# The first layer's weights are normalised after the values product; their reciprocals are widened, transposed and multiplied into the context

## The reference

```python
q = hidden @ Wq + bq                      # 32 heads of 16
k = enc @ Wk + bk; v = enc @ Wv + bv      # 8 key/value heads of 16
attn = softmax(q k^T / sqrt(16) + mask)
out = (attn @ v) @ Wo + bo
x = layer_norm(out + hidden) * gamma + beta
```

## Time and profile before

| what | value |
|---|---|
| median of three runs | 2440.0 us |
| the profiled execution | 2442.29 us, of which the span on the core is 2440.3 |
| busy TensorE, its weight loads | 2361.1 us (97%), 2030.8 us (83%) |
| busy VectorE, ScalarE, GpSimd | 1215.0 (50%), 868.8 (36%), 814.0 (33%) us |
| chain that ended last | TensorE 86%, GpSimd 7%, VectorE 3%, ScalarE 2% |
| granted TensorE clock | 0.992 of full speed |

### The profile page before, as it was taken

One profiled execution on the slowest core, in us unless ns is written; L12 is line 12 of the kernel. 1 busy time (PEld: TensorE's weight loads), 2 busy tenths in 40 slices (PEclk: granted clock), 3 DMA queues, 4 the chain that ended last, 5 costly groups with the idle time before them and its releaser, 6 DMA issues.

```text
span 2440.3 us, 38739 instructions
## 1 busy us (share of the span) xinstructions
PE 2361.1 (97%) x14768; PEld 2030.8 (83%) x14768; DVE 1215.0 (50%) x2041; ACT 868.8 (36%) x2501; POOL 814.0 (33%) x597
## 2 busy tenths in 40 slices
PE   7998999999999999999988899999999999999999
PEld 5777888888888888878866788888888888887887
DVE  6985333434533334465679843343354333334654
ACT  7964222222422222342379532222233222223321
POOL 6964232233322223130059442233243322322100
PEclk9999999999999999999999999999999999999999
DMA  5002111112110101211320021111111110110110
GB/s 206 10 10 83 35 43 52 37 48 67 35 35 34 43 34 43 74 44 61 115 85 6 10 83 44 48 46 52 34 57 35 36 41 34 43 52 14 61 44 35
DMA packets 37764, 120.06 MB, mean 49 GB/s; under 512 B 3616, under 2 KB 3872, under 8 KB 37664
## 3 DMA queue, kind: packets, MB, share of 16 engines
q1 hardware_dynamic: 37664, 118.69, 14.0%
HBM read 114.48 MB, written 4.19 MB: 49 GB/s over the span
## 4 chain that ended last, share of the span: by engine, by line
PE 86%; POOL 7%; DVE 3%; ACT 2%; issue 2%; DMA 0%; SPq 0%; POOLq 0%; DVEq 0%; ACTq 0%
PE PS L574 72%; PE PS L803 5%; PE PS L819 4%; PE PS L811 2%; POOL XN L429 1%; POOL W L453 1%; POOL HF L429 1%; POOL X L463 1%; POOL P0D L429 1%; POOL XN L422 1%; ACT AT L1147 1%; PE PS L794 1%; POOL W L386 1%; ACT PS L1147 1%; PE PS L839 0%
## 5 line engine op out<-in xcount | busy, mean ns | idle before, releaser
L574 PE MATMUL PS<-AT,W 128*128 128x512 f32 x2496 | 603.6, 392 | 7.1 <-DVE AT L1441 6.9
L574 PEld LDWEIGHTS PS<-AT,W 128*128 128x128 f32 x2496 | 467.8, 189 | 110.2 <-DVE AT L1441 9.8
L492 POOL TENSOR_TENSOR PR<-PR,RC 128x512 f32<-128x512 f32 x128 | 133.5, 1043 | 979.3 <-DVE RC L1528 979.3
L1320 DVE TENSOR_TENSOR X<-PS,X 128x512 f32<-128x512 f32 x416 | 286.0, 690 | 295.5 <-PE PS L574 288.4
L574 PE MATMUL PS<-CT,W 128*128 128x512 f32 x1632 | 408.9, 399 | 10.9 <-DVE CT L1315 10.5
L574 PE MATMUL PS<-W,CX 128*128 128x512 f32 x1632 | 397.2, 397 | 6.7 <-DVE Q L1345 4.0
L574 PE MATMUL PS<-W,CT 128*128 128x256 f32 x3072 | 385.9, 284 | 0.0
L574 PEld LDWEIGHTS PS<-W,CT 128*128 128x128 f32 x3072 | 372.9, 191 | 1.3 <-issue 0.8
L574 PEld LDWEIGHTS PS<-W,CX 128*128 128x128 f32 x1632 | 299.9, 188 | 74.0 <-issue 7.1
L574 PEld LDWEIGHTS PS<-CT,W 128*128 128x128 f32 x1632 | 298.8, 189 | 69.8 <-issue 11.6
L1174 ACT ACTIVATE CX<-PS,VEC 128x512 fp32r<-128x512 f32 x128 | 88.1, 689 | 660.9 <-PE PS L819 660.8
(11 more groups left out here) (110 smaller groups left out, 2462.0 us busy)
## 6 DMA issues: line engine op xcount, KB each, us to landing
RAW<-in_wq SPq DMA_DIRECT2D x44, 512.0 KB, 4.5
RAW<-in_wo SPq DMA_DIRECT2D x44, 512.0 KB, 3.2
RAW<-in_wk SPq DMA_DIRECT2D x40, 512.0 KB, 3.3
RAW<-in_wv SPq DMA_DIRECT2D x40, 512.0 KB, 3.4
raw_c<-in_cT SPq DMA_DIRECT2D x8, 512.0 KB, 6.0
raw_x<-in_xT SPq DMA_DIRECT2D x8, 512.0 KB, 5.7
BVR<-in_bv_rows SPq DMA_DIRECT2D x8, 512.0 KB, 3.6
X<-in_x SPq DMA_DIRECT2D x4, 1024.0 KB, 11.1
```

Of the source, the lines that this page charges most:

```text
L492: nc.gpsimd.tensor_tensor(PR[:, :, 0:P], PR[:, :, 0:P], RC[:, 0, 0:BT].unsqueeze(2).to_broadcast([P, BT, P]), ALU.mult).then_inc(norm_done, 1)
L574: ins = nc.tensor.matmul(out, lhs(c, a), rhs(c, b), start=(k == 0), stop=(k == total - 1))
L1320: V_.tensor_tensor(X[:, tile, :], PS[:, bank, :], X[:, tile, :], ALU.add).then_inc(done, 1)
```

## The change

In layer 0, GpSimd no longer multiplies the exponentials by the reciprocals before their transposition. The exponentials are transposed as they are. GpSimd adds the two halves of each of the last three heads (`half`), so that VectorE's sum over them reads 192 numbers a row and not 384, and it widens the eight reciprocals to 128 columns (`widen`), which TensorE transposes (`rt0`) into columns 256 to 383 of a score bank. When a unit's context has been evicted raw (`cxraw0`), VectorE multiplies it by the four transposed reciprocals (`cxnorm0`), and GpSimd makes its high and low part (`context`); for the last unit ScalarE and VectorE do (`last_cxlo0`). The value bias is added when the values are evicted. `RC` and `SUM0` have four slots, not two; the widened reciprocals and half sums lie in the upper half of the value-bias rows. The additions to X go between mask addition and maximum; `rec0` moves behind `soft0`; rows, bias tiles, quarters, the first keys and values of the next layer and the layer norm's first parts go to other steps. The diff, cut:

```diff
-    12: (2, (0,)), 13: (2, (1,)), 14: (2, (2,)), 15: (2, (3,)), 20: (1, (0, 1)), 21: (1, (2, 3)),
-    22: (3, (0,)), 23: (3, (1,)), 24: (3, (2, 3)), 25: (0, (0,)), 26: (0, (1,)), 27: (0, (2,)), 28: (0, (3,))}
+    11: (2, (0,)), 13: (2, (1,)), 15: (2, (2,)), 16: (2, (3,)), 17: (1, (0,)), 18: (1, (1,)), 20: (1, (2,)), 21: (1, (3,)),
+    23: (3, (0, 1)), 24: (3, (2, 3)), 26: (0, (0,)), 27: (0, (1,)), 28: (0, (2,)), 29: (0, (3,))}
-BO_AT = {8: 0, 9: 1, 10: 2, 11: 3, 16: 4, 17: 5, 18: 6, 19: 7}
-ROWS_AT = {9: (0, 0), 10: (0, 1), 11: (0, 2), 13: (0, 3), 17: (1, 0), 18: (1, 1), 19: (1, 2), 21: (1, 3),
-   25: (2, 0), 26: (2, 1), 27: (2, 2), 28: (2, 3)}
+BO_AT = {8: 0, 9: 1, 10: 2, 11: 3, 12: 4, 13: 5, 16: 6, 20: 7}
+ROWS_AT = {10: (0, 0), 11: (0, 1), 13: (0, 2), 14: (0, 3), 18: (1, 0), 19: (1, 1), 21: (1, 2), 22: (1, 3),
+   26: (2, 0), 27: (2, 1), 28: (2, 2), 29: (2, 3)}
...
+CXF = in_arena("CXF", [P, 3, 2, BTOK], F32, 36864)
...
+HS = BVR[:, 1024:1024 + (KV0 - OWN) * P].rearrange("p (s h t) -> p s h t", s=2, t=P // 2)
+RC0 = BVR[:, 1536:2048].rearrange("p (s n) -> p s n", n=P)
...
-        def norm(s):
+        def half(s):
+            pool.wait_ge(exp0, hf * STEPS0 + (s + 1))
+            if s >= 2:
+                pool.wait_ge(rc0, hf * STEPS0 + (s - 1))
+            z = P0[s % BUFS0].rearrange("p (h t) -> p h t", t=P)[:, OWN:KV0, :]
+            nc.gpsimd.tensor_tensor(HS[:, s % 2, :, :], z[:, :, 0:P // 2], z[:, :, P // 2:P], ALU.add).then_inc(half0, 1)
+        def widen(s):
             pool.wait_ge(rc0, hf * STEPS0 + (s + 1))
-            z = P0[s % BUFS0].rearrange("p (h t) -> p h t", t=P)
-            nc.gpsimd.tensor_tensor(z, z, RC[:, s % 2, :].unsqueeze(2).to_broadcast([P, KV0, P]),
-                                    ALU.mult).then_inc(norm0, 1)
+            if s >= 4:
+                pool.wait_ge(rt_ps, hf * STEPS0 + (s - 3))
+            copy_hi(RC0[:, s % 4, :].rearrange("p (h d) -> p h d", d=HD0),
+                    RC[:, s % 4, :].unsqueeze(2).to_broadcast([P, KV0, HD0])).then_inc(wide0, 1)
+        def context(u):
+            pool.wait_ge(cx0_n, hf * UNITS0 + (u + 1))
+            copy_hi(CX0[:, u % 3, 0, :], CXF[:, u % 3, 1, :]).then_inc(cx0_hi, 1)
+            pool.wait_ge(cx0_hi, hf * UNITS0 + (u + 1))
+            nc.gpsimd.tensor_tensor(CX0[:, u % 3, 1, :], CXF[:, u % 3, 1, :], CX0[:, u % 3, 0, :].bitcast(F32),
+                                    ALU.subtract).then_inc(cx0_lo, 1)
 
...
         sub(2)
+        half(0)
         for s in range(STEPS0):
-            if s + 1 < STEPS0:
-                norm(s + 1)
             if s == STEPS0 - 2:
                 sub_rows(0, 0)
             if s + 3 < STEPS0:
                 sub(s + 3)
+            if s + 1 < STEPS0:
+                half(s + 1)
+            widen(s)
+            if s % 4 == 1 and s > 1:
+                context(s // 4 - 1)
             if s in BO_AT:
...
         def t0(s):
-            pe.wait_ge(norm0, s0 + (s + 1))
+            pe.wait_ge(exp0, s0 + (s + 1))
...
             elif b == 0:
-                pe.wait_ge(cx0_lo, u0 + u)
+                pe.wait_ge(cx0_raw, u0 + u)
...
+        def rt0(s, bank, col):
+            pe.wait_ge(wide0, s0 + (s + 1))
+            nc.tensor.transpose(PS[:, bank, col:col + P], RC0[:, s % 4, :],
+                                IDENT[:]).then_inc(rt_ps, 1)
...
                 pv0(s - 1)
+            if s and s <= STEPS0 - 4:
+                pe.wait_ge(z0, s0 + (s + 4))
+                if s % 4 == 1 and s > 1:
+                    pe.wait_ge(cx0_n, u0 + s // 4)
+                rt0(s - 1, B0 + (s - 1) % 4, 256)
             if s + 4 < STEPS0:
                 s0_(s + 4)
...
             if s in ROWS_AT:
                 out0(s)
-            if s == STEPS0 - 4:
-                pe.wait_ge(z0, s0 + STEPS0)
+            if s == STEPS0 - 3:
+                pe.wait_ge(cx0_n, u0 + UNITS0 - 1)
                 keys(n1, 0, 0, w1, BS)
-            if s == STEPS0 - 3:
+            if s == STEPS0 - 2:
                 values(n1, 0, w1, None, (0, 1))
-            if s == STEPS0 - 2:
+            if s == STEPS0 - 1:
                 values(n1, 0, w1, None, (2, 3))
-            if s == STEPS0 - 1:
-                keys(n1, 0, 1, w1, BS + 1)
+        keys(n1, 0, 1, w1, BS + 1)
...
+        pe.wait_ge(cx0_lo, u0 + UNITS0 - 1)
         last_rows0(0, 0)
+        pe.wait_ge(xadd, x0 + 3 * BT)
         last_rows0(1, 0)
         pv0(STEPS0 - 1)
+        for t in range(BT):
+            rt0(STEPS0 - BT + t, BPV, t * P)
         pe.wait_ge(k_ev, n1 * 2 + 2)
         last_rows0(2, 0)
...
-            nc.scalar.activation(VT[:, tb, :], PS[:, BB, :], ACT.Copy).then_inc(vt_ev, 1)
+            nc.scalar.activation(VT[:, tb, :], PS[:, BB, :], ACT.Identity, bias=VEC[:, COL_BV0:COL_BV0 + 1]).then_inc(vt_ev, 1)
...
         def e0(s):
...
-            if s >= 2:
-                act.wait_ge(rc0, s0 + (s - 1))
+            if s >= 4:
+                act.wait_ge(rc0, s0 + (s - 3))
...
-                                     bias=MX[:, s % BUFS0, h:h + 1], accum_out=SUM0[:, s % 2, h:h + 1])
+                                     bias=MX[:, s % BUFS0, h:h + 1], accum_out=SUM0[:, s % 4, h:h + 1])
...
-        def cxhi0(u):
+        def cxraw0(u):
...
-            nc.scalar.activation(CX0[:, u % 3, 0, :], PS[:, BB, :], ACT.Identity,
-                                 bias=VEC[:, COL_BV0:COL_BV0 + 1]).then_inc(cx0_hi, 1)
+            nc.scalar.activation(CXF[:, u % 3, 1, :], PS[:, BB, :], ACT.Copy).then_inc(cx0_raw, 1)
...
             if s == 0:
...
             if s % 4 == 0 and s:
-                cxhi0(s // 4 - 1)
+                cxraw0(s // 4 - 1)
             if s + 3 < STEPS0:
...
-            if s == STEPS0 - 4:
+            if s == STEPS0 - 3:
                 first_keys(0, BS)
-            if s == 30:
+            if s == 31:
                 root(hf * 8)
         first_keys(1, BS + 1)
-        cxhi0(UNITS0 - 1)
+        cxraw0(UNITS0 - 1)
+        act.wait_ge(cx0_n, u0 + UNITS0)
+        nc.scalar.activation(CX0[:, (UNITS0 - 1) % 3, 0, :], CXF[:, (UNITS0 - 1) % 3, 1, :], ACT.Copy).then_inc(cx0_hi, 1)
         root(hf * 8 + 1)
...
-        def soft0(s):
+        def soft0(s, row=None):
...
+            if row is not None:
+                row0(row)
             dve.wait_ge(z0, s0 + (s + 1))
             V_.tensor_reduce(MX[:, s % BUFS0, :], P0[s % BUFS0].rearrange("p (h t) -> p h t", t=P),
                              AXX, ALU.max, negate=True).then_inc(max0, 1)
...
+        def row0(s):
+            n, t = ROWS_AT[s]
+            if n < 2:
+                dve.wait_ge(bo_tile, hf * SEQ + (n * BT + t + 1))
+            add0(n, t, BA)
...
-            V_.tensor_reduce(SUM0[:, s % 2, OWN:KV0], P0[s % BUFS0].rearrange("p (h t) -> p h t", t=P)[:, OWN:KV0, :],
-                             AXX, ALU.add).then_inc(sum0, 1)
-            if s >= 2:
-                dve.wait_ge(norm0, s0 + (s - 1))
+            dve.wait_ge(half0, s0 + (s + 1))
+            V_.tensor_reduce(SUM0[:, s % 4, OWN:KV0], HS[:, s % 2, :, :], AXX, ALU.add).then_inc(sum0, 1)
+            if s >= 4:
+                dve.wait_ge(wide0, s0 + (s - 3))
...
-            V_.reciprocal(RC[:, s % 2, :], SUM0[:, s % 2, :]).then_inc(rc0, 1)
-        def cxlo0(u):
-            dve.wait_ge(cx0_hi, u0 + (u + 1))
-            V_.scalar_tensor_tensor(CX0[:, u % 3, 1, :], PS[:, BB, :], VEC[:, COL_BV0:COL_BV0 + 1],
-                                    CX0[:, u % 3, 0, :].bitcast(F32), ALU.add, ALU.subtract).then_inc(cx0_lo, 1)
+            V_.reciprocal(RC[:, s % 4, :], SUM0[:, s % 4, :]).then_inc(rc0, 1)
+        def cxnorm0(u):
+            dve.wait_ge(cx0_raw, u0 + (u + 1))
+            if u < UNITS0 - 2:
+                dve.wait_ge(s0_ps, s0 + (4 * u + 9))
+            else:
+                dve.wait_ge(rt_ps, s0 + (4 * u + 4))
+            rt = PS[:, B0:B0 + 4, 256:256 + P] if u < UNITS0 - 1 else PS[:, BPV, :].rearrange("p (b t) -> p b t", t=P)
+            cx = CXF[:, u % 3, 1, :].rearrange("p (b t) -> p b t", t=P)
+            V_.tensor_tensor(cx, rt, cx, ALU.mult).then_inc(cx0_n, 1)
+        def last_cxlo0():
+            u = UNITS0 - 1
+            dve.wait_ge(cx0_hi, u0 + UNITS0)
+            V_.tensor_tensor(CX0[:, u % 3, 1, :], CXF[:, u % 3, 1, :], CX0[:, u % 3, 0, :].bitcast(F32),
+                             ALU.subtract).then_inc(cx0_lo, 1)
...
         soft0(1)
-        rec0(0)
...
         for s in range(STEPS0):
-            if s + 1 < STEPS0:
-                rec0(s + 1)
...
-                cxlo0(s // 4 - 1)
+                cxnorm0(s // 4 - 1)
             if s - 2 in Q_AT:
                 qlo0(Q_AT[s - 2])
+            row = s - 1 if s - 1 in ROWS_AT else None
             if s + 3 < STEPS0:
-                soft0(s + 3)
+                soft0(s + 3, row)
+            elif row is not None:
+                row0(row)
+            rec0(s)
             if s == 0:
                 klo0(1)
-            if s - 1 in ROWS_AT:
```

(41 more changed lines are left out.)

## The result

| kernel | median us | lowest to highest | ratio to before | span, granted clock of the profiled execution |
|---|---|---|---|---|
| before | 2439.8 | 2439.55 to 2441.57 (4) | | 2440.3, 0.992 |
| after | 2458.7 | 2458.15 to 2459.63 (4) | 1.0076 [1.0064, 1.0089] | 2456.3, 0.994 |

The change makes the kernel 18.9 us slower by the medians, 16.0 by the spans of the two profiled executions. The forecast was 2438, with 2446 as its upper end.

A forecast was written before the change was run, and what follows sets the result against it. GpSimd was taken to bound layer 0's step loop. Per half, 5.2 us gained by transposition 28 less 4.2 lost in the tail gives 1.0, so 2.0 off the 2440.0 median: 2438 us, range 2428 to 2446.

The forecast's parts named there:

- Outside this loop and its tail the change touches nothing.: Scope claim: only layer 0's step loop and its tail change in time; no cost was set for the rest.
- The paragraph on what costs nothing: Priced at no cost: bias on evicted values, buffers in the value-bias rows, weight quarters at other steps.
- the two signs of being wrong: Tail's TensorE wait under 1 us (then faster), or transposition 28 less than 3 us sooner (then slower).
- GpSimd sets the pace, and no longer does: Layer 0's loop, steps 8 to 27: GpSimd's work falls from 80.7 to 69.3 us, busy share from 98 to 85-90%.
- Prologue 0.7, transposition 8 3.4 sooner, transposition 28 5.2: Layer 0's loop: time gained by each point, earlier gains included; transposition 1 to 28 about 102.5 us, from 107.4.
- A small transposition at 0.12, an eighth of eight: TensorE, each step: the new 128-column transposition of wide reciprocals costs 0.12 us, an eighth of a step's 0.97.
- The lumps make `widen` late: GpSimd's loop queue: context, bias tile and quarter, up to 6.1 us with the step's work, delay `widen`; 3.3 us lost.
- four engines stand within 2% of each other: Layer 0's loop, steps 8 to 27: GpSimd, TensorE, ScalarE and VectorE each need about 70 us; queue order settles the gain.
- The tail 4.2 longer: After transposition 28, per half: an extra row 1.5 us, later root making TensorE wait 2.85 instead of 0.46, small transpositions.
- the third rival: TensorE's clock: 4 us of work at 1.2 GHz in loop or tail costs 2 us per half, 2442; chance 0.08.
- the forecast's own case: Whole program: the forecast itself holds, 2434 to 2442 us, chance 0.45.
- Sum, 1.0 gained per half: Per half: 5.2 us gained in the loop less 4.2 lost in the tail; 2.0 gained in the program.

The follow-up runs named there:

- the padding alone: The kernel before with one unused tensor of 128 bytes a partition ahead of the arena, nothing else: 2453.85 us, ratio 1.0051.
- the address put back: The changed kernel with its two four-slot tables RC and SUM0 laid behind the arena, so the arena stands where it was before: 2446.54 us, ratio 1.0023.

## Why the prediction was wrong

- **The step that failed is "Outside this loop and its tail the change touches nothing."** It touches every address in the arena. The paragraph on what costs nothing lists the buffers laid into the value-bias rows and not the two tables that grow; the diff shows both. It was never priced, and it costs 12.6 us (the padding alone), two thirds of the 18.9. No row of before shows that a distance matters, since its two large products stand at quick ones; but "what moved in memory" was not on the list of what could go wrong, and so no rival held it and the range ended 12.7 us too low. With the address put back the kernel has 2446.5, half a microsecond past the range's end. Neither of the two signs of being wrong that the prediction names came (a tail wait under 1 us, transposition 28 less than 3 us sooner), for both look only into layer 0.
- *GpSimd sets the pace, and no longer does: right.* 85% busy against 85 to 90 predicted. `half` takes 0.60 us (0.59 predicted), `widen` 0.31 (0.3), the context's parts 0.62 and 1.28 (0.62 and 1.28). The groups of GpSimd between 30 and 170 us in the changed kernel, columns as in the earlier trace rows:

```profile
L390 POOL TENSOR_SCALAR BVR<-RC 128x128 f32<-128x128 f32 x32 | 10.0, 313 | 0.6 <-DVE RC L1415 0.6
...
L450 POOL TENSOR_TENSOR CX<-CXF,CX 128x512 fp32r<-128x512 f32 x7 | 9.0, 1284 | 0.6
L435 POOL TENSOR_TENSOR BVR<-HF 128x192 f32<-128x192 f32 x8 | 4.8, 598 | 0.0
L390 POOL TENSOR_SCALAR CX<-CXF 128x512 fp32r<-128x512 f32 x7 | 4.4, 622 | 0.0
```

- *Prologue 0.7, transposition 8 3.4 sooner, transposition 28 5.2: nearly right.* 1.7 at transposition 1, 2.7 at transposition 8 (64.59 against 67.30), 4.7 at 28. The 107.4 became 104.5 and not 102.5. By the prediction's own terms it should have read 102.9, since 0.7 of the 5.2 lies ahead of transposition 1; another 1.0 came ahead of it than was reckoned, and 0.5 was not gained. The size of the gain up to transposition 28 was nearly the forecast's; where it arose was not.
- *A small transposition at 0.12, an eighth of eight: wrong by two.* From its start to the next one's it is 0.23 to 0.26 us, mostly 0.26:

```profile
82.21 0.33 PE L719 MATMUL PS<-IDENT,BVR 128*128 128x128 f32 x1
82.47 0.62 PE L686 MATMUL PS<-KZ,Q 32*128 32x256 f32 x12
```

  28 of them are up to 3.9 us more TensorE time than reckoned, in a loop where TensorE has waits of 2.9 us for `widen` and 3.5 for VectorE beside them. How much of the 3.9 was on the path, no run separates.
- *The lumps make `widen` late: right as a wait, unsure as a price.* 2.9 us on TensorE, where 3.3 of the loop's loss was set down to GpSimd's lateness at four places. But 1.6 of it taken away in the first half shortened the loop there by 0.4 only. That fits the sentence that four engines stand within 2% of each other: when one is no longer late, another nearly is.
- *The tail 4.2 longer: right in mechanism, short in size.* The one wait is 2.80, 2.85 predicted (the prediction's own times, 27.65 less 24.9, give 2.75). The tail lost 5.7; the difference of 1.5 is the clock's fall behind that very wait (4.61 - 3.02 = 1.6 us). This was the third rival, at 2 us a half and a chance of 0.08, and by these runs it is a part of the forecast's own case rather than a rival to it, for the slow matmuls came every time with the wait that the forecast had. The Trainium skill (TensorE: Matmul & The Clock Gate, What's actually happening) has the throttled state as the default that activity releases. The traces agree: behind waits of 0.46, 0.85, 1.25, 1.26 and 2.10 us the twelve matmuls took 3.0 to 3.1, behind waits of 2.80 to 2.85 they took 4.61 four times and 5.49 twice, counting both halves of each trace. That the loop would have fewer such stretches is borne out in part: of the twelve loops in the six traces of the new order, two in each, eight ran at 1.00 and four at 0.97 or 0.98, where the kernel before had 0.95 and 0.98.
- *Sum, 1.0 gained per half:* measured 1.0 lost in the first and 2.1 in the second, in all some 3 lost where 2.0 were to be gained (what the address costs inside layer 0 is in this and wasn't separated); so without the address the forecast would have been 5 us off, of which some 3.2 are the clock in two tails. The medians of the kernel with the address put back say more, 5.3 over the kernel before in the same runs (2446.54 against 2441.26): its runs spread over 8 us, those of before over 2 to 5. Lower clock in the loop can be part of that, at some 2.4 us a loop. The kernel before has such stretches too, and it seems that its GpSimd hid them: its loop takes 107.4 us at 0.94 to 0.95 and 107.6 at 0.98.

## What to carry to other kernels

When a table grows ahead of others, write down which operands moved, and compare the time of a matmul group that the change does not touch between the two traces: a difference of 0.1 us in 24 matmuls was worth more here than everything that the change meant to do. Allocate what may grow behind the big operands. And where a step is moved later, follow what waits for its smallest instruction (here a root of 0.21 us, with a table load of 1.28 ahead of it). If a wait of TensorE like the 2.8 us here comes out, count the matmuls behind it at the lower clock too.

## What the runs showed of the hardware

- The pace of a product of 128x512 matmuls that moves `W` and has its stationary tile in the arena changes with the arena's position, and goes back when the arena is moved by 256 bytes or when all ahead of it moves too. By the distance of the two tiles modulo 256 bytes it is 226.8 and 227.6 ns a matmul at 0, 228.9 at 192, 233.3 at 64 in both products, 232.9 at 128. A product with neither operand in the arena changed as well, by 1.2 ns a matmul, so the distance of the operands can't be the whole cause. The Trainium skill (SBUF — State Buffer, SBUF: two separate sides) says that on the engines' side "only the shared port pair causes contention", and that is the pair of VectorE and GpSimd. That doesn't account for this: the one tile of padding changed no instruction of any engine, only addresses, and TensorE's busy time went up by 12.5 us (2361.1 to 2373.6).
- A lone transposition of 128 columns between other kinds of matmul costs 0.23 to 0.26 us from start to start; in a row of eight it is 0.97 for all.
